# Second expert matmul with w2 as the loaded weights, and results transposed back

## What is computed

```python
# E=8 experts, 2 picked per token, capacity 320 slots per expert and batch, F=448
dispatch = einsum('bsm,bsec->ebcm', hidden_states, dispatch_mask)
h1 = einsum('ebcm,emh->ebch', dispatch, w1)
h3 = einsum('ebcm,emh->ebch', dispatch, w3)
expert_out = einsum('ebch,ehm->ebcm', silu(h1) * h3, w2)
final = einsum('ebcm,bsec->bsm', expert_out, combine_mask)   # weights: softmax of the router
```

## Time and profile before

| | |
|---|---|
| runs (3) | 890.52, 893.83 (median), 895.33 us |
| profiled execution | 894.59 us |
| its span, first to last instruction | 892.7 us |
| mean granted TensorE clock | 0.95 of full speed |
| TensorE busy | 779.4 us, 87% |
| VectorE, ScalarE, GpSimd busy | 504.7, 520.3, 338.3 us |
| `results` L1408, TensorE busy | 118.7 us, 768 passes |
| `hidden` L1378, TensorE busy | 120.7 us, 384 passes |

### The profile page before, as it was taken

The page is one execution under the profiler, slowest core; times in us unless marked ns, Lnnn a source line. Parts: engine busy times, 40 slices in busy tenths (PEclk is TensorE's granted clock), DMA queues, the critical chain, the costliest instruction groups (busy, mean ns, idle before and its releaser), DMA issues. The chain is left out here.

```text
span 892.7 us, 14333 instructions
## 1 busy us (share of the span) xinstructions
PE 779.4 (87%) x4780; PEld 445.4 (50%) x4780; DVE 504.7 (57%) x1365; ACT 520.3 (58%) x805; POOL 338.3 (38%) x345
## 2 busy tenths in 40 slices
PE   2599999989999969999989887989989887999992
PEld 1332222212223226766656665766657765777771
DVE  6777433216563138733565489897788845533341
ACT  4367997979999958532555547547565323433330
POOL 4070003301000442375322676766754730574332
PEclk9899999989999989999999998999889969999997
DMA  4021745318810110113100200000000010122212
GB/s 125 1 72 63 180 110 122 94 58 256 191 55 19 33 43 23 37 52 94 48 21 13 59 1 0 2 1 1 2 1 1 29 47 17 49 70 70 63 42 83
DMA packets 61862, 50.26 MB, mean 56 GB/s; under 512 B 10460, under 2 KB 53585, under 8 KB 61528
## 3 DMA queue, kind: packets, MB, share of 16 engines
q1 hardware_dynamic: 56376, 40.50, 17.1%
q0 software_dynamic: 5120, 8.68, 3.0%
q10 hardware_dynamic: 288, 0.10, 0.1%
HBM read 26.55 MB, written 23.81 MB: 56 GB/s over the span
## 5 line engine op out<-in xcount | busy, mean ns | idle before, releaser
L633 ACT ACTIVATE attn_p<-attn_ps 128x1024 f32<-128x1024 f32 x256 | 240.5, 1051 | 28.2 <-PE attn_ps L648 20.6
L648 PE MATMUL attn_ps<-attn_p,attn_v 128*32 128x512 f32 x1024 | 139.1, 611 | 1.8 <-issue 1.4
L1378 PE MATMUL ps_main<-moe_xsT,moe_w 128*128 128x320 f32 x384 | 120.7, 458 | 3.9 <-DVE moe_hid L1398 3.7
L1408 PE MATMUL ps_main<-moe_w,moe_hid 128*128 128x128 f32 (+3 forms) x768 | 118.7, 291 | 3.2 <-ACT mb_y L1417 3.2
L1408 PEld LDWEIGHTS ps_main<-moe_w,moe_hid 128*128 128x128 f32 (+3 forms) x768 | 95.4, 172 | 29.0 <-issue 9.3
L1398 DVE TENSOR_TENSOR moe_hid<-moe_act_h,ps_main 128x320 f32<-128x320 f32 (+1 forms) x128 | 62.0, 486 | 78.6 <-PE ps_main L1378 58.1
L1388 ACT ACTIVATE moe_act_h<-ps_main 128x320 f32<-128x320 f32 (+1 forms) x128 | 55.0, 434 | 86.2 <-PE ps_main L1378 56.1
L1312 POOL DMA_INDIRECT moe_slots<-rows,moe_scatter_at x64 | 63.4, 990 | 108.2 <-ACT attn_p L633 90.8
L626 PE MATMUL attn_ps<-attn_q_rows,attn_k_rows 64*128 64x512 bf16 x448 | 84.5, 389 | 12.0 <-ACT attn_p L633 5.5
L1424 POOL DMA_INDIRECT moe_rows<-moe_y,moe_dest x48 | 46.4, 966 | 114.6 <-ACT moe_y L1417 102.4
L1378 PEld LDWEIGHTS ps_main<-moe_xsT,moe_w 128*128 128x128 f32 x384 | 71.3, 196 | 35.3 <-issue 8.4
(11 more groups left out here) (225 smaller groups left out, 1327.2 us busy)
## 6 DMA issues: line engine op xcount, KB each, us to landing
moe_slots<-zeros SPq DMA_DIRECT2D x4, 1380.0 KB, 13.4
moe_w<-in_w SPq DMA_DIRECT2D x3, 1536.0 KB, 11.1
moe_xs<-moe_slots SPq DMA_DIRECT2D x32, 138.0 KB, 2.2
moe_rows<-zeros SPq DMA_DIRECT2D x4, 1024.0 KB, 15.7
moe_back<-moe_rows SPq DMA_DIRECT2D x16, 256.0 KB, 3.7
attn_q_rows<-attn_q_parts SPq DMA_DIRECT2D x56, 48.0 KB
attn_k_rows<-attn_k_parts SPq DMA_DIRECT2D x28, 96.0 KB
attn_q_parts<-attn_parts SPq DMA_DIRECT2D x6, 256.0 KB, 2.9
```

The source lines that it names most:

```text
L633: self.core.nc.scalar.activation(self.p[:, w % self.PB, :, :].rearrange("p a n -> p (a n)"), self.ps_s[:, w % self.SB, :, :].rearrange("p ...
L648: ins = self.core.nc.tensor.matmul(self.ps_av[32 * i:32 * i + 32, :], self.v[:, b * TPB + kt, HGROUPS * i + m, :], self.p[:, w % self.PB, ...
L1378: self.core.nc.tensor.matmul(ps[:, w % 2, 0:CAP], wt[:, e, c * P:(c + 1) * P], self.xsT[:, u % 2, :], start=True, stop=True).then_inc(self ...
L1408: ins = self.core.nc.tensor.matmul(self.ps_y[0:n, s * D:(s + 1) * D], self.hid[rows, u % 2, c, c0:c0 + n], self.w2[rows, u % E_, c, :], st ...
```

## The change

`results` now loads w2 as weights and moves `hid`: four matmuls of 320 columns per unit in place of twelve of 128. What comes out is transposed (features on partitions, slots along the free axis), so the router's weight can't be applied there. A new `keep` on ScalarE copies it from `ps_y` to the tile `yT` (lent by the mamba), a new `turn_back` on TensorE makes three transposes of `yT` into bank `ps_t`, which `turn` uses as well, and `weigh` reads them from `ps_t`.

The order changes too. On TensorE a unit is now hidden(u, 0), turn_back(u-2), hidden(u, 1), results(u-1), turn(u+1), hidden(u, 2), hidden(u, 3). On ScalarE weigh(u-2) follows silu(u, 0), and keep(u-1) follows silu(u, 1). On VectorE take(u+1) follows gating(u, 1). Work hung in at chunk 0 or 1 comes after these. So a unit's weigh and send happen in the second unit after it, not in the first. `turn` waits for the weigh that read `ps_t`, `turn_back` for the take that read it. The second half (units 16 to 31) is changed in the same way. The cuts (...) hold the same edits for the other half and the new first argument of the calls.

```diff
@@ -1334,10 +1335,14 @@
     def loaded(self, eng, u):
         eng.wait_ge(self.slots_in[u % self.RING], 32 * (u // self.RING + 1))
 
-    def turn(self, pe, u):
+
+
+    def turn(self, pe, u, y_before):
         self.loaded(pe, u)
         if u >= 1:
             pe.wait_ge(self.t_read, u)
+        if y_before:
+            pe.wait_ge(self.y_read, 3 * y_before)
         for s, (c0, n) in enumerate(self.CHUNKS):
             ins = self.core.nc.tensor.transpose(self.ps_t[:, c0:c0 + n], self.xs[0:n, u % self.RING, s, 0:D], self.core.ident[0:n, 0:n])
         ins.then_inc(self.turned, 1)
@@ -1401,20 +1406,35 @@
     def results(self, pe, u):
         pe.wait_ge(self.gated, FCH * (u + 1))
         if u >= 1:
+            pe.wait_ge(self.y_kept, u)
+        for c in range(FCH):
+            rows = slice(0, P) if c < FCF else self.REST_ROWS
+            ins = self.core.nc.tensor.matmul(self.ps_y[:, 0:CAP], self.w2[rows, u % E_, c, :], self.hid[rows, u % 2, c, :],
+                                             start=(c == 0), stop=(c == FCH - 1))
+        ins.then_inc(self.y_done, 1)
+
+    def keep(self, act, u):
+
+        act.wait_ge(self.y_done, u + 1)
+        if u >= 1:
+            act.wait_ge(self.y_turned, u)
+        self.core.nc.scalar.copy(self.yT, self.ps_y[:, 0:CAP]).then_inc(self.y_kept, 1)
+
+    def turn_back(self, pe, u, turns_before):
+        pe.wait_ge(self.y_kept, u + 1)
+        pe.wait_ge(self.t_read, turns_before)
+        if u >= 1:
             pe.wait_ge(self.y_read, 3 * u)
         for s, (c0, n) in enumerate(self.CHUNKS):
-            for c in range(FCH):
-                rows = slice(0, P) if c < FCF else self.REST_ROWS
-                ins = self.core.nc.tensor.matmul(self.ps_y[0:n, s * D:(s + 1) * D], self.hid[rows, u % 2, c, c0:c0 + n], self.w2[rows, u % E_, c, :],
-                                                 start=(c == 0), stop=(c == FCH - 1))
-        ins.then_inc(self.y_done, 1)
+            ins = self.core.nc.tensor.transpose(self.ps_t[0:n, s * D:(s + 1) * D], self.yT[:, c0:c0 + n], self.core.ident[:])
+        ins.then_inc(self.y_turned, 1)
 
     def weigh(self, act, u):
 
-        act.wait_ge(self.y_done, u + 1)
+        act.wait_ge(self.y_turned, u + 1)
         act.wait_ge(self.sent, u + 1)
         for s, (c0, n) in enumerate(self.CHUNKS):
-            self.core.nc.scalar.activation(self.y[u % self.OUT][0:n, s, :], self.ps_y[0:n, s * D:(s + 1) * D], ACT.Copy,
+            self.core.nc.scalar.activation(self.y[u % self.OUT][0:n, s, :], self.ps_t[0:n, s * D:(s + 1) * D], ACT.Copy,
                                            scale=self.weight[0:n, u % self.OUT, s:s + 1]).then_inc(self.y_read, 1)
 
     def send(self, pool, u):
@@ -1927,6 +1947,7 @@
         main = ctx.enter_context(nc.psum_tensor("ps_main", [P, 6, BANK], F32))
         moe.open(ctx, "moe", main)
         mamba.open(ctx, "mb", norm.xT, norm.side, main)
+        moe.yT = mamba.e_seg[:, 1, :, :].rearrange("p h t -> p (h t)")[:, 0:CAP]
         moe.y += [lent.rearrange("p a c t -> p (a c t)")[:, 0:3 * D].rearrange("p (s d) -> p s d", s=3) for lent in (mamba.y2[:], mamba.y_old[:])]
 
         ffn = FfnOfBatch(core, B + 1, 12, mamba.act_t[:, 1, :, :].rearrange("p c (h t) -> p (c h) t", h=2)[:, 0:6, :])
...
@@ -1947,12 +1968,18 @@
                 for u in range(HALF):
                     if u == E_:
                         moe.results(pe, u - 1)
-                        moe.turn(pe, u)
-                    if u + 1 < HALF and u + 1 != E_:
-                        moe.turn(pe, u + 1)
+                        moe.turn_back(pe, u - 2, u)
+                        moe.turn(pe, u, u - 1)
                     for c in range(FCH):
                         if u or c:
                             moe.hidden(pe, u, [c])
+                        if c == 0 and u >= 2 and u != E_:
+                            moe.turn_back(pe, u - 2, u + 1)
+                        if c == 1:
+                            if u and u != E_:
+                                moe.results(pe, u - 1)
+                            if u + 1 < HALF and u + 1 != E_:
+                                moe.turn(pe, u + 1, max(u - 1, 0))
 
                         if u == 3 and c < 2:
                             ffn.output(pe, c)
@@ -1971,15 +1998,15 @@
                     if u == 4:
                         pe.wait_ge(norm.ready, 16)
                         moe.logits(pe, 1)
-                    if u and u != E_:
-                        moe.results(pe, u - 1)
                     if u == 11:
                         pe.wait_ge(norm.ready, 18)
                         mamba.steps(pe, 0)
                     if 11 <= u < 15:
                         mamba.project(pe, 0, u - 11)
+                moe.turn_back(pe, HALF - 2, HALF)
                 moe.results(pe, HALF - 1)
                 mamba.project(pe, 0, 5)
+                moe.turn_back(pe, HALF - 1, HALF)
                 pe.wait_ge(moe.y_read, 3 * HALF)
                 pe.wait_ge(mamba.norm_done, 1)
                 mamba.before(pe, 0)
...
@@ -2039,11 +2073,9 @@
                             moe.logits(pe, 3)
                         if u == HALF + 3 and c == 0:
                             moe.counts(pe, 3)
-                    if u == HALF + 1:
-                        pe.wait_ge(mamba.out_read, PARTS_OUT * UNITS)
-                    if u > HALF:
-                        moe.results(pe, u - 1)
+                moe.turn_back(pe, 2 * HALF - 2, 2 * HALF)
                 moe.results(pe, 2 * HALF - 1)
+                moe.turn_back(pe, 2 * HALF - 1, 2 * HALF)
 
             @block.sync
             def _(sp):
@@ -2106,10 +2138,10 @@
                         ffn.take(dve)
                     if u == E_:
                         moe.take(dve, u)
-                    if u + 1 < HALF and u + 1 != E_:
-                        moe.take(dve, u + 1)
                     for c in range(FCH):
                         moe.gating(dve, u, [c])
+                        if c == 1 and u + 1 < HALF and u + 1 != E_:
+                            moe.take(dve, u + 1)
 
                         if u < 3:
                             for h in share(UNITS_AT[u], c):
...
@@ -2218,8 +2250,15 @@
                 for i in (12, 13):
                     norm.copy(act, nc.scalar.copy, i)
                 for u in range(HALF):
+                    if u == E_:
+                        moe.keep(act, u - 1)
+                        moe.weigh(act, u - 2)
                     for c in range(FCH):
                         moe.silu(act, u, [c])
+                        if c == 0 and u >= 2 and u != E_:
+                            moe.weigh(act, u - 2)
+                        if c == 1 and u and u != E_:
+                            moe.keep(act, u - 1)
 
                         if u < 3:
                             for h in share(UNITS_AT[u], c):
@@ -2250,11 +2289,11 @@
                             mamba.silu_rows(act, 0, range(2))
                         if u == 15 and c == 3:
                             mamba.take(act, 0, 4)
-                    if u:
-                        moe.weigh(act, u - 1)
                     if 11 <= u < 15:
                         mamba.take(act, 0, u - 11)
                         mamba.first_tap(act, 0, u - 11)
+                moe.weigh(act, HALF - 2)
+                moe.keep(act, HALF - 1)
                 moe.weigh(act, HALF - 1)
                 mamba.silu_rows(act, 0, range(2, 4))
                 mamba.take(act, 0, 5)
...
```

More of the change, by code:

```diff
@@ L1209, in open @@
         self.ps_t, self.ps_h1, self.ps_h3, self.ps_y = main[:, 0, :], main[:, 1:3, :], main[:, 3:5, :], main[:, 5, :]
+        self.y_kept, self.y_turned = sem("y_kept"), sem("y_turned")
         self.tail_clear, self.chain = sem("tail_clear"), sem("chain")
@@ L1941, in _ @@
                 core.landed(pe, "moe_gate", "ident", "moe_w1", "moe_w3", "moe_w2", "mb_w_dt", "mb_w_xbc", "mb_w_z")
-                moe.turn(pe, 0)
+                moe.turn(pe, 0, 0)
                 for i in (12, 13):
@@ L2024, in _ @@
                 mamba.output(pe, UNITS - 1, 0)
-                moe.turn(pe, HALF)
+                moe.turn(pe, HALF, HALF)
                 for u in range(HALF, 2 * HALF):
-                    if u + 1 < 2 * HALF:
-                        moe.turn(pe, u + 1)
                     for c in range(FCH):
                         moe.hidden(pe, u, [c])
+                        if c == 0 and u >= HALF + 2:
+                            moe.turn_back(pe, u - 2, u + 1)
+                        if c == 1:
+                            if u == HALF + 1:
+                                pe.wait_ge(mamba.out_read, PARTS_OUT * UNITS)
+                            if u > HALF:
+                                moe.results(pe, u - 1)
+                            if u + 1 < 2 * HALF:
+                                moe.turn(pe, u + 1, max(u - 1, HALF))
                         if u == HALF and c in (1, 3):
@@ L2187, in _ @@
                 for u in range(HALF, 2 * HALF):
```

(12 more changed lines are left out.)

## The result

The changed kernel took 882.37 us (median of 4 runs, 881.16 to 884.68), the kernel before 894.25 us beside it (4 runs, 890.52 to 895.33): a ratio of 0.9866, 95% interval 0.9819 to 0.9914, or -12 us (-16 to -8). Predicted were 884.9 us, 877 to 893, and 0.70 for faster. The profiled execution took 881.57 us, with a span of 879.6.

A forecast was written before the change was run, and what follows sets the result against it. TensorE's queue was taken to bound the longest stretch. Halves of -3.7 and -6.2 us gave -9.9, plus 1.0 for clock -8.9: 894.59 to 885.7 profiled, 884.9 for the runs' median, range 877 to 893.

The forecast's parts named there:

- The unit: Undisturbed expert unit: 8.06 us falls to 7.62, with results at 2.20 and three transposes back at 0.50; bounds 7.40 and 7.75.
- The wait for the third gating: Between quiet units: the next unit's first pair waits for the third pair's gating, so a unit gains 0.44 us, not 0.92.
- Rival A: Quiet units: the new wait between units does not bite, units cost 7.14 us, program 878.7 us; chance 0.12.
- 442.9 to 494.3: First-half stretch with 5.3 us of TensorE idle: mid-unit results cover all but about 2.4, and the stretch gains 7.0 us.
- Rival B: In 442.9 to 494.3 ScalarE's chain replaces TensorE's idle, the 7.0 us don't come, program 891.9 us; chance 0.17.
- Unit 5: Stretch 347.5 to 385.3: the counting matmuls wait 3.0 us for picked, and the stretch gives back 2.8 us.
- Unit 10 and 11: Stretch 422.5 to 442.9: TensorE waits 2.7 and 1.0 us for gatings behind combine and statistics blocks; +0.7 us.
- The clock term: Whole program: the two new waits of about 3 us may cost granted clock; 1.0 us added.
- rival C: Added idle and transposes lower TensorE's clock; decides from 13.4 us, some eight more slow stretches; slower, chance 0.10.
- Halves: Sums of the stretches: first half -3.7 us, second half -6.2 us.
- Rival D: Results: w2 as weights does not stream, eight passes cost 3.4 us instead of 2.2, program about 900 us; chance 0.04.
- Turn(8): Unit 8's turn, waiting for slots filled by GpSimd's 16 scatters, which start 3.6 us later; turn 3 to 4 us later.

The follow-up runs named there:

- rest_full: The changed kernel with each unit's fourth result matmul over 128 rows instead of 64, the added rows zeroed; 878.95 us, ratio 0.9821 to the kernel before.
- end_order: The changed kernel's operands in the old order: turn and take at the unit's top, results at its end; 898.42 us, ratio 1.0042 to the kernel before.
- mixed: The changed kernel, second half only: results at the unit's end, turn at its top, turning back behind the second chunk; 885.92 us, ratio 0.9887 to the kernel before.
- after again: The changed kernel, unchanged, profiled a second time; 891.09 us.
- after: The first profiled execution of the changed kernel; 881.57 us.
- counts_late: The changed kernel with the routing's counting matmuls of units 5 and 19 behind the second chunk, not the first; 886.04 us, ratio 0.9884 to the kernel before.
- few_scatters: The changed kernel with counting matmuls behind the second chunk and eight of the second routing's sixteen scatters left out; 921.38 us on a slower chip, ratio 0.976.
- combined: The changed kernel with full-row results, second half's results at unit end, turning back behind chunk two, unit 24's turn late; 922.07 us, slower chip, ratio 0.9767.
- keep_twice: The changed kernel with ScalarE's copy of the results made twice; 937.50 us on a slower chip, ratio 0.9912 to the kernel before.

## Why the prediction was right, point by point

- **The unit** was forecast at 7.62 us and measured at 7.66, with two errors that cancel. Results: 2.20 predicted, 2.44 measured; the step that failed is "The columns, not the weight loads, set the pace of such passes", right within one shape. It rests on a pace of 0.151 us for 128 columns, and that is a mean of 0.11 and 0.20: the extra time comes at a change of shape (rest_full). Turning back: 0.50 taken between 0.33 and 0.60, measured 0.32, just under the lower end. That the two nearly cancel, +0.24 and -0.18, is luck.
- **The wait for the third gating**, forecast as what turns a gain of 0.92 into 0.44, is there in every quiet unit, and its timing was right: from the third pair's start to the next unit 2.13 us forecast (5.49 to 7.62), 2.09 measured (818.42 to 820.51). Rival A (no such wait) falls. end_order and mixed, with quiet units of 7.2, show that it is worth 0.45 us a unit.
- **442.9 to 494.3**: 44.4 us forecast, 44.5 measured. Rival B falls: the new order covers TensorE's idle time there (1.5 us left, at results(15); 2.4 forecast).
- **775.6 to 863.7**: -4.3 forecast, -3.9 measured. 741.0 to 756.7: -2.7 forecast, -2.7 measured.
- **Unit 5** is the step that was mis-sized most: 347.5 to 385.3 was to give back 2.8 us and gave back 4.9. The wait was right (2.88 for 3.0); the clock behind it was not in the term. The slow pair cost 1.2 us and the results 0.3 more; in after again the results there took 4.20. The slow pair is there in all three executions of these instructions (after, after again, mixed).
- **Unit 10 and 11**: waits of 1.88 and 1.39 us (2.7 and 1.0 forecast), then a pair and the results at the lower clock (2.27 and 3.81 us for 1.08 and 2.44): 422.5 to 442.9 lost 3.0 us, not 0.7. This is chance of one execution: in after again and in mixed the same instructions wait 1.88 and 1.53 us, every pass behind runs at its usual pace, and from turn(11) to turn(12) they take 11.10 us, not 13.58. There the stretch loses about what was forecast.
- **756.7 to 775.6**: +1.5 forecast, +4.0 measured, two slow pairs at its head among it.
- **The clock term**, 1.0 us in all, is thus the term that failed: the slow pairs and results of units 5 and 11 alone make 4.0 us in the profiled execution; unit 5's 1.5 to 3.0 us, which come each time, already exceed the whole term. The prediction named new dips of the clock as a sign that it is wrong, and three stretches show them (0.96, 0.85 and 0.91 for 1.00), though the time came out as forecast. In direction this is rival C. It stayed far below the 13.4 us from which C decides, since the clock stayed at 1.00 in the long quiet stretches despite six transposes a unit.
- **Halves.** First -3.7 forecast, -1.1 measured; second -6.2 and -6.7. The sum of -7.8 from the four profiles lies at the edge of the -8 to -16 of the timed runs, and mixed's first half would make it -9.0; with stages that vary by several us between executions, the profiles don't settle the rest. That the forecast of -8.9 lies within 3 us of the measured -12 says no more than that.
- **Rival D** falls: w2 as weights streams at 0.27 us a pass.
- **Turn(8)** was the other thing said to come late: +3.6 forecast, +4.4 measured against before's turn, 1.8 us of different start taken into account. counts_late shows the wall of the first half: where the units ahead of it are shorter (counts_late, end_order, rest_full), turn(8) waits 6.46, 7.38 and 4.36 us for its rows and comes 82.7 to 83.7 us behind turn(0), as in after (82.5). In after again and mixed it waits 1.4 us for ScalarE's weighing instead, so the changed kernel as it stands only just meets the wall. That the sixteen scatters make it rests on their rows and their 1.28 us; the run meant to test that, few_scatters, doesn't.

What stays open is what makes those passes slow. counts_late took wait and slow passes away together in unit 5, which fits a loss that follows the wait. But in rest_full the same wait of 2.88 us had a pair and results of the usual length behind it (381.25 to the next turn at 384.78), while combined, with the same first half, had the slow pair (2.27 us) behind it; keep_twice had the usual pair. So four of six executions with this wait lose. In after the wait of 2.69 us in unit 19 cost nothing either. No run takes the waits away and leaves the rest.

## What to carry to other kernels

Price a swap of operands together with its order: each alone lost here, and both together gained, because the order decides whether the added step waits. The new order is not the only one: combined keeps the old order in its second half, moves only the turning back behind the second chunk, and has the shortest quiet unit. Where an engine has idle time before a late transfer, ask first when that transfer can come at all; five microseconds saved ahead of unit 8 were worth nothing while GpSimd issued 19 indirect DMAs at 1.28 us. Keep the tiles of a run of matmuls in one shape: zero rows cost nothing, one spell of another shape 0.35 us a unit. And try that first: the kernel before has three such spells, and filling them alone was not measured.

## What the runs showed of the hardware

- A spell of two passes with 64 weight rows in a run with 128 makes three steps longer by 0.09 to 0.10 us each, with passes of 128 columns (0.20 to 0.21 for 0.11, before) as with passes of 320 (0.36 to 0.37 for 0.27, after). The idle time of the weight loads, 0.44 us on either side in after, is longer than what reaches the unit's length: 0.28 us in the results and 0.07 in the turn.
- Behind a wait of 2.88 us a pair took 2.27 us in place of 1.08 in some executions and not in others. Waits of 0.2 us in every quiet unit left the granted clock at 1.00.
- The same kernel took 5.6% longer on one chip than on others (945.57 against 895.50 us). In the combined kernel there, the second half has a row with 13.70 us of idle time and no releaser (811.22), and VectorE's and ScalarE's instructions stand for 14.11 and 10.88 us as well, while GpSimd's scatters go on at 1.28 us each:

```profile
806.41 0.43 ACT L1422 COPY mb_e_seg<-ps_main 128x320 f32<-128x320 f32 x1 [10.88 <-remote]
810.63 0.49 DVE L1357 COPY moe_xsT<-ps_main 128x320 f32<-128x320 f32 x1 [14.11 <-remote]
811.22 0.87 PE L1430 MATMUL ps_main<-ident,mb_e_seg 128*128 128x128 f32 x3 [13.70 <-issue]
```

Such stretches lie beside the scatters in both halves, in few_scatters too (7.80 us at 405.91); what holds the three engines is not shown.
